# The FFN of a four-batch Mamba and attention block: fc1 over two halves of the tokens, residual and bias added on GpSimd and VectorE

## What is computed

```
x = x + attn_out * gamma1
x2 = _ln(x) * (scale2 + 1.0) + shift2
h = gelu(x2 @ fc1_w.T + fc1_b)            # exact gelu, 256 -> 1024
ffn_out = h @ fc2_w.T + fc2_b             # 1024 -> 256
x = x + ffn_out * gamma2
```

## Time and profile before

| | us |
|---|---|
| median of 3 runs | 3235.7 |
| lowest, highest | 3234.0, 3252.0 |
| the profiled execution, its span from first to last instruction | 3238.7 |
| busy in it: PE, VectorE, ScalarE, GpSimd | 3165.7, 2754.9, 2711.7, 2447.2 |

### The profile page before, as it was taken

The page is one execution under the profiler, slowest core; times in us unless marked ns, Lnnn a source line. Parts: engine busy times, 40 slices in busy tenths (PEclk is TensorE's granted clock), DMA queues, the critical chain, the costliest instruction groups (busy, mean ns, idle before and its releaser), DMA issues.

```text
span 3238.7 us, 59471 instructions
## 1 busy us (share of the span) xinstructions
PE 3165.7 (98%) x23272; PEld 2625.2 (81%) x23272; DVE 2754.9 (85%) x3077; ACT 2711.7 (84%) x4528; POOL 2447.2 (76%) x621
## 2 busy tenths in 40 slices
PE   7999999999999999999999999999999999999999
PEld 6998899884699889987479989998648998888844
DVE  3999999966399999996549999999656999999862
ACT  4999999955599999994569999999357999999744
POOL 2999999950199999994039999999305999999800
PEclk9999999999999999999999999999999999999999
DMA  5222322210222222220022222223002222222100
GB/s 187 72 87 68 89 68 84 87 42 1 74 66 87 79 85 74 80 88 30 9 75 72 88 83 74 86 69 92 15 14 79 84 77 84 69 74 81 48 14 7
DMA packets 194232, 222.02 MB, mean 69 GB/s; under 512 B 77336, under 2 KB 149016, under 8 KB 193056
## 3 DMA queue, kind: packets, MB, share of 16 engines
q1 hardware_dynamic: 193952, 218.22, 21.9%
HBM read 213.70 MB, written 4.48 MB: 67 GB/s over the span
## 4 chain that ended last, share of the span: by engine, by line
PE 82%; POOL 8%; issue 4%; DVE 3%; ACT 1%; DMA 1%; SPq 0%; DVEq 0%; ACTq 0%; POOLq 0%
PE bank L1053 22%; PE bank L1033 17%; PE bank L1034 10%; PE bank L933 7%; POOL states L627 5%; PE bank L1029 4%; PE bank L1252 4%; PE bank L1125 3%; POOL y_gated L627 3%; PE bank L1273 2%; PE bank L1285 2%; PE bank L1171 2%; PE bank L1352 2%; DVE states L1509 1%; PE bank L1060 1%
## 5 line engine op out<-in xcount | busy, mean ns | idle before, releaser
L627 POOL TENSOR_TENSOR states<-states,c_rows 128x2048 f32<-128x2048 f32 x336 | 1532.8, 4582 | 411.8 <-DVE states L1509 396.2
L1509 DVE TENSOR_TENSOR_SCAN states<-decay,bank 128x512 f32<-128x512 f32 x1376 | 1576.7, 1201 | 126.1 <-PE bank L1034 111.1
L780 ACT ACTIVATE decay<-dt,a_log 128x512 f32<-128x512 f32 x2048 | 1305.4, 710 | 0.0
L771 ACT ACTIVATE inflow_tok<-dtx_tok,b_tok 128x512 f32<-128x512 f32 x1536 | 995.5, 712 | 69.9 <-PE bank L1034 61.0
L1033 PE MATMUL bank<-ident,inflow_tok 128*128 128x128 f32 x5280 | 904.4, 280 | 36.6 <-DVE states L1509 18.1
L1053 PE MATMUL bank<-ident,states 128*128 128x128 f32 x5504 | 825.2, 273 | 4.4 <-DVE y_gated L1515 3.0
L1509 DVE TENSOR_TENSOR_SCAN y_gated<-decay,bank 128x512 f32<-128x512 f32 x672 | 776.3, 1201 | 12.9 <-ACT decay L780 5.5
L627 POOL TENSOR_TENSOR y_gated<-y_gated,c_rows 128x2048 f32<-128x2048 f32 x168 | 770.0, 4584 | 19.9 <-DVE y_gated L1509 18.1
L1033 PEld LDWEIGHTS bank<-ident,inflow_tok 128*128 128x128 f32 x5280 | 599.1, 141 | 207.6 <-issue 90.4
L1034 PE MATMUL bank<-b_diag,dtx_tok 128*128 128x128 f32 x3520 | 681.0, 275 | 0.0
L1053 PEld LDWEIGHTS bank<-ident,states 128*128 128x128 f32 x5504 | 645.3, 142 | 11.3 <-DVE y_gated L1515 5.3
(11 more groups left out here) (166 smaller groups left out, 2513.1 us busy)
## 6 DMA issues: line engine op xcount, KB each, us to landing
c_rows<-c_spill SPq DMA_DIRECT2D x256, 512.0 KB, 3.7
b_diag<-diag_ring SPq DMA_DIRECT2D x256, 128.0 KB, 2.2
xproj_w<-in_xproj_w SPq DMA_DIRECT2D x32, 320.0 KB, 3.9
in_w<-in_in_w SPq DMA_DIRECT2D x16, 512.0 KB, 4.6
in_w<-in_fc_w SPq DMA_DIRECT2D x8, 512.0 KB, 4.5
xproj_w<-in_w SPq DMA_DIRECT2D x8, 512.0 KB, 4.6
xproj_w<-in_fc_w SPq DMA_DIRECT2D x4, 1024.0 KB, 4.8
x_ahead<-in_x SPq DMA_DIRECT2D x4, 512.0 KB, 6.4
```

The lines of the kernel that those rows point to most:

```text
L627: pool.tensor_tensor(state_row, state_row, c_row.to_broadcast([P, KI, L]), ALU.mult).then_inc(weighed, PAIRS)
L771: last_tok = act.activation(inflow_tok[:, r % SLOTS, t, :], dtx_tok[:, d, t, :], ACT.Copy, scale=b_tok[:, d, t, s:s + 1])
L780: act.activation(decay[:, r % SLOTS * KI + k, :], dt[:, d, k, :], ACT.Exp, scale=a_neg[:, d, k, s:s + 1]).then_inc(decay_ready, 1)
L1509: dve.tensor_tensor_scan(state_slots[r % STATES][:, k, time], decay[:, slot, time], banks[k % INFLOW_BANKS][:, time], 0.0, ALU.mult, ALU.a ...
```

## The change

Three things change in the FFN, and with them the counts of some semaphores. In fc1, each of the 8 tiles is computed in two halves of the tokens. PE turns and pads only the first two tiles of the LayerNorm, then runs half 0 (tokens 0 to 255) of all eight m, with the turns of tiles 2 and 3 behind m = 0 and m = 2, and then half 1 of all eight. The banks are taken in the order 4, 5, 0, 1, 2, 3, 6, 7; a bank below 4 waits for the copy out of it alone, and banks 6 and 7 for the last tile's shift. In fc2, token tile 0 waits for each gelu in turn in place of all at the start, and no tile has anything put into its bank before. The residual and the bias leave PE: GpSimd multiplies the fc2 bias by gamma2 on all partitions and adds it to `x_att` once the copies are there (`att_biased`), and VectorE adds PSUM and `x_att` into `x_out` tile by tile (`out_ready`), in place of ScalarE's copies. The waits of SyncE and of PE's next batch that hung on those copies hang on `out_ready`. The helper `add_rows` keeps its use in the attention projection.

Left out of the diff are the declarations of the new semaphores and three places where PE waits on the renumbered counts (the copies of the second LayerNorm, `proj_gated`, and the next batch's first `sum_up`, which now waits for `out_ready`).

```diff
--- before.py
+++ after.py
@@ -63,6 +63,8 @@
 OUT_BANK = 4
+FC1_BANKS = (4, 5, 0, 1, 2, 3, 6, 7)
+FC1_TURN_AT = {0: 2, 2: 3}
 KEEP = 2
@@ -224,7 +226,7 @@
         proj_g = x_in[:, 0:KD, :]
-        bias_g = x_in[0:1, KD:KD + 2, :]
+        bias_g = x_in[:, KD:KD + 2, :]
         after_inflow = inflow_tok[:].rearrange("p a t c -> p (a t) c")
@@ -575,7 +580,7 @@
                         load_xproj(1, kc)
-                sp.wait_ge(res_copied, (b + 1) * 3 * TT)
+                sp.wait_ge(out_ready, (b + 1) * TT)
                 sp.dma_start(out_rows[b], x_out[:]).then_inc(out_stored, 16)
@@ -673,12 +678,17 @@
                                    ALU.mult).then_inc(proj_gated, 1)
-                for i, (g, bias) in enumerate([(GAMMA1, PROJ_B), (GAMMA2, FC2_B)]):
-                    pool.tensor_tensor(bias_g[:, i, :], row_b[0:1, bias, :], gate[0:1, g, :], ALU.mult).then_inc(proj_gated, 1)
+                pool.tensor_tensor(bias_g[0:1, 0, :], row_b[0:1, PROJ_B, :], gate[0:1, GAMMA1, :], ALU.mult).then_inc(proj_gated, 1)
+                pool.tensor_tensor(bias_g[:, 1, :], row_b[:, FC2_B, :], gate[:, GAMMA2, :], ALU.mult).then_inc(bias_ready, 1)
...
                                    ALU.mult).then_inc(fc2_gated, 1)
+
+                pool.wait_ge(bias_ready, b + 1)
+                pool.wait_ge(res_copied, (b + 1) * 2 * TT)
+                pool.tensor_tensor(x_att[:], x_att[:], bias_g[:, 1, :].unsqueeze(1).to_broadcast([P, TT, D]),
+                                   ALU.add).then_inc(att_biased, 1)
@@ -713,8 +723,7 @@
                 if i:
-                    bank = banks[OUT_BANK + t if i == 3 else t]
-                    act.activation(x_of[i + 1][:, t, :], bank[:, 0:D], ACT.Copy).then_inc(res_copied, 1)
+                    act.activation(x_of[i + 1][:, t, :], banks[t][:, 0:D], ACT.Copy).then_inc(res_copied, 1)
@@ -864,14 +873,11 @@
                     act.wait_ge(fc1_mm, b * KF + m + 1)
-                    act.activation(gelu_h[:, m, :], banks[(m + KH) % KF], ACT.Gelu, bias=fc1_b[:, m:m + 1]).then_inc(fc1_ready, 1)
+                    act.activation(gelu_h[:, m, :], banks[FC1_BANKS[m]], ACT.Gelu, bias=fc1_b[:, m:m + 1]).then_inc(fc1_ready, 1)
                 if not last:
...
                     feed_scan(b + 1, 1)
-                for t in range(TT):
-                    act.wait_ge(res_mm, (b * RES + 3) * TT + t + 1)
-                    copy_rows(b, 3, t)
@@ -1114,15 +1120,15 @@
-            def add_rows(t, x, bias=None, at=0):
-
-                pe.matmul(banks[at + t][:, 0:D], ident[:], x[:, t, :], start=True, stop=False)
+            def add_rows(t, x, bias=None):
+
+                pe.matmul(banks[t][:, 0:D], ident[:], x[:, t, :], start=True, stop=False)
                 if bias is not None:
-                    pe.matmul(banks[at + t][:, 0:D], ident[0:1, 0:1].to_broadcast([1, P]), bias_g[:, bias, :], start=False, stop=False)
-
-            def residual_tile(t, lhs, rhs, steps, at=0):
+                    pe.matmul(banks[t][:, 0:D], ident[0:1, 0:1].to_broadcast([1, P]), bias_g[0:1, bias, :], start=False, stop=False)
+
+            def residual_tile(t, lhs, rhs, steps):
                 for c in range(steps):
-                    last = pe.matmul(banks[at + t][:, 0:D], lhs(c, t), rhs(c), start=False, stop=(c == steps - 1))
+                    last = pe.matmul(banks[t][:, 0:D], lhs(c, t), rhs(c), start=False, stop=(c == steps - 1))
                 last.then_inc(res_mm, 1)
@@ -1343,22 +1349,37 @@
                     residual_tile(t, lambda c, t: o_t[:, c, t * P:(t + 1) * P], lambda c: proj_g[:, c, :], KD)
-                ln(b, 3)
+                def fc1_half(m, half):
+
+                    for kc in range(KD):
+                        last = halves(banks[FC1_BANKS[m]], fc1_w[:, kc, m * P:(m + 1) * P], h_t[:, kc, :], (half,),
+                                      kc == 0, kc == KD - 1)
+                    return last
+
+                for t in range(2):
+                    ln_turn(b, 3, t)
+                    for _ in range(KEEP):
+                        pe.matmul(banks[O_BANK][:, 0:D], ident[:], qkv_w[:, 0, 0:D], start=True, stop=True)
                 pe.wait_ge(fc1_loaded, 16 * KD * (b + 1))
+                ln_wait(b, 3, 1)
                 for m in range(KF):
-                    if m == KH:
-                        pe.wait_ge(res_copied, (b * 3 + 2) * TT)
-                    for kc in range(KD):
-                        last = pe.matmul(banks[(m + KH) % KF], fc1_w[:, kc, m * P:(m + 1) * P], h_t[:, kc, :],
-                                         start=(kc == 0), stop=(kc == KD - 1))
-                    last.then_inc(fc1_mm, 1)
-                for t in range(TT):
-                    pe.wait_ge(fc1_ready, b * KF + t + 1)
-                    add_rows(t, x_att, 1, OUT_BANK)
+                    if FC1_BANKS[m] < TT:
+                        pe.wait_ge(res_copied, (b * 2 + 1) * TT + FC1_BANKS[m] + 1)
+                    if FC1_BANKS[m] >= LN_BANK:
+                        ln_wait(b, 3, TT - 1)
+                    fc1_half(m, 0)
+                    if m in FC1_TURN_AT:
+                        ln_turn(b, 3, FC1_TURN_AT[m])
+                for m in range(KF):
+                    fc1_half(m, 1).then_inc(fc1_mm, 1)
                 pe.wait_ge(fc2_gated, b + 1)
-                pe.wait_ge(fc1_ready, (b + 1) * KF)
-                for t in range(TT):
-                    residual_tile(t, lambda c, t: gelu_h[:, c, t * P:(t + 1) * P], lambda c: fc2_w[:, c, :], KF, OUT_BANK)
+                for t in range(TT):
+                    for c in range(KF):
+                        if t == 0:
+                            pe.wait_ge(fc1_ready, b * KF + c + 1)
+                        last = pe.matmul(banks[OUT_BANK + t][:, 0:D], gelu_h[:, c, t * P:(t + 1) * P], fc2_w[:, c, :],
+                                         start=(c == 0), stop=(c == KF - 1))
+                    last.then_inc(res_mm, 1)
@@ -1637,6 +1658,10 @@
                 summed_ln(b, 2, EPS_LN)
+                dve.wait_ge(att_biased, b + 1)
+                for t in range(TT):
+                    dve.wait_ge(res_mm, (b * RES + 3) * TT + t + 1)
+                    dve.tensor_tensor(x_out[:, t, :], banks[OUT_BANK + t][:, 0:D], x_att[:, t, :], ALU.add).then_inc(out_ready, 1)
...
```

11 lines of the change are left out of this document (7 added, 4 removed).

## The result

| | us |
|---|---|
| median of the kernel before, 4 runs beside it | 3234.8 (3232.7 to 3252.0) |
| median of the changed kernel, 4 runs | 3210.2 (3209.9 to 3214.5) |
| ratio, with its 95% interval | 0.991 (0.989 to 0.993) |
| the profiled execution: its span, its time | 3208.1, 3209.9 |

The changed kernel is faster by 24.6 us, or 0.9%. The forecast was 3204, the range 3197 to 3220; the measured median lies in the range, 6.2 above the forecast. A span is 1.7 to 1.8 us shorter than the time of the same execution, in each profile for which both are on record.

The account below looks back on a forecast made before the run. PE was taken to bound the FFN stage end to end. Four times 6.86 us (27.44), plus 6.54 of clock, less 0.1 at the tail, took 33.9 off 3238.7: 3204.8, stated as 3204 us, range 3197 to 3220.

Parts of the forecast that it names:

- What bounds the stage: FFN stage ending each batch: PE's from end to end, so every us off its queue moves the next batch forward.
- Part 1: Start of fc1: it begins after two turned tiles, gaining 2.56 us a batch; two turns among the halves cost 0.54.
- Part 2: fc1: 64 half-width records at 0.217 us each take 13.91 us, 0.07 more than the 32 whole ones.
- (c): Rival, fc1: half-width records cost 0.307 us, giving 23 us back, so 3228 and no difference; chance 0.06.
- (d): Rival, fc1: a half costs what a whole does, 0.4325 us a record, so slower at 3260; chance 0.03.
- Rival (b): fc1's start: late copies or shifts, or 14 new waits each exposing a 0.19 us weight load; 3215; chance 0.09.
- Part 3: Between fc1 and fc2: 16 residual and bias records leave PE, 4.91 us a batch; GpSimd's and VectorE's additions hide.
- Part 4: fc2 follows fc1 without a wait and ends 6.86 us earlier a batch; nothing later gives the gain back.
- rival (e): Start of fc2: still waits for all gelus, at most 0.9 us a batch, 3208; chance 0.62 together with the forecast.
- rival (a): FFN stage or close behind: the clock falls all the same, 3211, or 3218 with one in each batch; chance 0.20.
- Part 5: FFN stage, batches 0 and 2: both clock drops go with the one-row bias and identity matmuls, 6.54 us.
- The sum: Whole kernel: 27.44 plus 6.54 less 0.1 is 33.9 us off the profiled 3238.7, giving 3204.8.

Follow-up runs that it names:

- e1: The changed kernel, but with fc1 whole as before, behind all four LayerNorm turns; 3216.8 us, ratio 0.992.
- e3: The kernel before with the fc1 halves and the early start alone, residual and bias staying on PE; 3232.3 us, ratio 0.997.
- e10: The changed kernel with 16 useless records between fc1 and fc2, full-row and one-row matmuls taking turns; 3232.3 us, ratio 0.997.
- e8: The changed kernel with 16 useless full-row records between fc1 and fc2; 3220.3 us, ratio 0.994.
- e2: The changed kernel, but with all eight gelus awaited ahead of fc2; 3213.2 us, ratio 0.991.
- e7: The changed kernel with 16 useless one-row records between fc1 and fc2; 3232.9 us, ratio 0.997.
- e4: The kernel before with FFN and attention-projection bias rows added by full 128-row identity matmuls, same number of records; 3222.3 us, ratio 0.995.
- e9: The changed kernel with the attention-projection bias also added by GpSimd and the value bias made full-row; 3205.2 us, ratio 0.989.

## Why the prediction was right, point by point

**What bounds the stage.** Right. PE was the bound end to end before, and is after: the 34.5 us of PE's queue in the stage left the span, up to what falls outside.

**Part 1, the early start.** Right. The gain was 4.93 less 2.46, 2.47 for 2.56. fc1 starts 0.15 us after the second tile's shift and not 0.05: the shifts begin at 1617.05 and take 0.81, fc1 begins at 1618.01. A turn costs 0.22 (1619.16 less 1618.94) for 0.27. Net of the turns and of part 2 it is worth 1.98 where the prediction has 1.95, and e1 and e3 show it alone.

**Part 2, the halves.** Right: 0.216 us a record, 0.217 said. Rivals (c), a record at 0.307, and (d), a half at the cost of a whole, fall with it. So does the estimate of 3 to 14 us a batch more that the prediction worked out from the figures of the Trainium skill, page "TensorE: Matmul & The Clock Gate", section "Back-to-back issue gap": e1 against after shows 0.06 us for the step from 32 to 64 records. Rival (b), an early start that is eaten by waits or exposed loads, falls too. None of the 14 waits shows in the timeline.

**Part 3, residual and bias.** The sum is right: 4.91 gone, GpSimd's addition 2.35 for 2.3, VectorE's 0.42 for 0.48, hidden with 0.19 to spare for 0.3. That 0.307 is the fair end of a range for any 256-column record was wrong as a reading of the earlier trace rows. It is 0.216 and the price of full-row and one-row matmuls taking turns (e10: 4.91, e8: 3.45), which fc1's halves never do.

**Part 4, fc2 at once.** Right on its first half: no wait ahead of fc2's tiles, and the stage 6.99 shorter where 6.86 was said. 0.10 of the difference is fc2: its 13.91 in the earlier trace rows held the record that comes 0.10 late behind the last one-row matmul, and went to 13.81 with it, just under the 13.9 to 14.1 that was to show it. e2 sizes the edit on which this hung: with fc2 behind all gelus, as rival (e) had it, 1.11 a batch are lost, a little over the 0.9 that the prediction gave it. The sentence that nothing gives the gain back did not hold. What lies outside the stage was put at 0 and measured 3.8 us between the two profiles. 2.4 of it are the fall of the clock in the scan of batch 3, which both profiles of the changed kernel have. It is a fall of the clock as in rival (a), but in a place that (a) does not name, a batch's scan away. The other 1.4 are less than the two profiles of the kernel before differ there (almost 7), and say nothing of the change.

**Part 5, the clock.** The effect is right: both falls went, 6.54 expected, and batches 0 and 2 gained 3.29 and 3.25 more than batch 1. That there were two was the luck of that profile; the next one of the same kernel has three. The cause was half right. It is the one-row matmuls (e7 against e8), not the identity ones (e4). e4 also shows that the change was not needed for this: the kernel before with full-row bias rows holds the clock as well.

**The sum.** From the profile's 3238.7 the prediction took 33.9 and came to 3204.8. Two terms and the baseline were off. The stage gave 34.5 and not 34.0 (with the tail's 0.1, 33.9), and outside it 3.8 came back: 3204.8 - 0.5 + 3.8 = 3208.1, which is the span after. The baseline is that 3238.7 is a span. Its time is not on record; if it is 1.8 more, as in the other profiles, the sum stood for 3206.6 in time, and the profile before stood 4.8 above the median of 3235.7 and not 3.0. But the changed kernel's runs lie closer together than those of the kernel before (3209.9 to 3214.5 against 3232.7 to 3252.0), since part of what scattered is gone, and the profiled time of after, 3209.9, is its median within 0.3. With the three of them, 3204.8 + 1.8 + 3.8 - 0.5, one comes to 3209.9. This is bookkeeping after the fact: the 3.8 could not have been worked out ahead, and it moves with the pair of profiles that one takes.

What stays open is why the clock falls in the scan of batch 3 of the changed kernel and in none of the other twelve profiles, at a place where PE is idle a third of the time in before, after and e1, and why its falls in the scores come and go in length from one batch and one profile to the next. No run here changed what PE does in either place alone, beyond e9's step, which settled nothing.

## What to carry to other kernels

Where one engine bounds a stage, price each edit by rows of the same form in the same stage (here the terms met 34 us within 0.5), and leave an amount for the clock elsewhere: outside the stage three profiles with the same instructions lie up to 9 us apart, a quarter of the gain. Before moving a broadcast bias off PE, try it there with full-row operands; done for the FFN and for the attention projection, which the change leaves alone, that was worth 17.0 us where the change was worth 30.2 beside the same runs. And look for which work covers which wait before taking work away: the rows removed here had hidden the last gelu, so 1.0 us of their 4.9 a batch came only with the finer waits.

## What the runs showed of the hardware

- An fp32 record costs by its columns, with a new 128x128 weight for each matmul: 0.216 us at 256 columns (64 in 13.81), 0.432 at 512 (32 in 13.83).
- A one-row matmul costs what a full-row one costs: 0.216 us a record for 256 columns (e7 in a row, e8). A change between the two costs 0.19 to 0.20 us each way, so matmuls that take turns come to 0.307 a record (4.91 for 16, e10).
- The granted clock fell from 2.4 to 1.2 GHz with PE busy all the time, behind 16 records of which 8 or all were one-row, in 10 of 20 stages; in 0 of 8 behind 16 full-row records, and in 0 of 36 without one-row records in all. Why not in all 20 stays open: the instructions of the stage were the same in each batch.
- GpSimd's fp32 addition of 128x1024 with a broadcast operand takes 2.35 us. VectorE's addition out of PSUM of 128x256 takes 0.42, and ScalarE's copy out of it 0.38.
